# Second attention layer of a graph network: the wait for the sums moved behind ScalarE's distances

## The reference, cut to what matters

```python
q = (h @ Wq + bq).reshape(n, HEADS, HEAD_DIM) * scaling
k = (h @ Wk + bk).reshape(n, HEADS, HEAD_DIM)
v = (h @ Wv + bv).reshape(n, HEADS, HEAD_DIM)
s = jnp.einsum('ehd,ehd->eh', q[row], k[col])
m = jax.ops.segment_max(s, row, num_segments=n)
p = jnp.exp(s - m[row])
denom = jax.ops.segment_sum(p, row, num_segments=n)
attn = p / denom[row]
out = jax.ops.segment_sum(attn[:, :, None] * v[col], row, num_segments=n)
```

## Time and profile before

| | |
|---|---|
| median of 3 runs | 9040.61 us (9038.01 to 9045.36) |
| profiled execution, its own time | 9037.91 us |
| its span, first to last instruction | 9036.1 us |
| busy share of the span | PE 69%, DVE 63%, ACT 27%, POOL 68% |
| mean granted TensorE clock over the span | 0.809 of full speed |
| second attention layer, first to last one-hots (L1469) | 5319.6 to 7633.4 us |

### The profile page before, as it was taken

The page is one execution under the profiler, slowest core; times in us unless marked ns, Lnnn a source line. Parts: engine busy times, 40 slices in busy tenths (PEclk is TensorE's granted clock), DMA queues, the critical chain, the costliest instruction groups (busy, mean ns, idle before and its releaser), DMA issues. The chain is left out here.

```text
span 9036.1 us, 124148 instructions
## 1 busy us (share of the span) xinstructions
PE 6249.3 (69%) x27682; PEld 3822.4 (42%) x27683; DVE 5729.5 (63%) x14736; ACT 2476.3 (27%) x7366; POOL 6125.2 (68%) x5632
## 2 busy tenths in 40 slices
PE   5100077777777775999999778888888887555554
PEld 2000044444444444444444445555555555334433
DVE  7000076666666665888888778888888887322223
ACT  0000044444444442333333223333333333000000
POOL 4777677777777774888888635555555555677772
PEclk8555577777777777999999889999999998777776
DMA  2000043333343342333233533333333344333354
GB/s 88 13 1 1 8 117 104 107 106 106 107 108 108 108 106 60 86 84 85 84 85 85 53 94 105 105 105 105 105 105 106 105 106 92 98 104 104 105 99 50
DMA packets 411759, 790.73 MB, mean 88 GB/s; under 512 B 198754, under 2 KB 228172, under 8 KB 411084
## 3 DMA queue, kind: packets, MB, share of 16 engines
q0 software_dynamic: 283584, 725.19, 31.8%
q1 hardware_dynamic: 128140, 65.15, 2.5%
HBM read 749.73 MB, written 40.22 MB: 87 GB/s over the span
## 5 line engine op out<-in xcount | busy, mean ns | idle before, releaser
L1787 POOL DMA_INDIRECT gat<-y,rec_sb_s x908 | 1218.7, 1342 | 276.5 <-issue 259.4
L1545 DVE TENSOR_REDUCE small<-ps 128x2 f32<-128x1024 f32 x900 | 1091.7, 1222 | 308.1 <-PE ps L1413 266.4
L907 POOL DMA_INDIRECT gat<-kv,rec_sb_d x912 | 988.3, 1084 | 302.1 <-issue 275.2
L1350 POOL DMA_INDIRECT gat<-kv,rec_sb_s x916 | 889.9, 971 | 403.6 <-issue 314.3
L2051 POOL DMA_INDIRECT gat<-x,rec_sb_d x908 | 863.1, 951 | 332.2 <-issue 265.0
L2065 PE MATMUL ps<-gat,oh 128*128 128x256 f32 x1792 | 664.4, 537 | 528.7 <-DMA gat<-x,rec_sb_d 402.5
L495 POOL DMA_INDIRECT rec_s<-wts,rows x784 | 836.5, 1067 | 238.9 <-issue 238.3
L434 POOL DMA_INDIRECT rec_d<-small x784 | 764.9, 976 | 335.2 <-issue 247.2
L1828 PE MATMUL ps<-big,oh 128*128 128x512 f32 x1792 | 960.7, 635 | 0.0
L1360 POOL TENSOR_TENSOR big<-gat,big 128x1024 f32<-128x1024 f32 x225 | 442.6, 1967 | 588.4 <-ACT big L1483 588.4
L989 PE MATMUL ps<-big,oh 128*128 128x264 f32 x1800 | 795.3, 558 | 0.4
(11 more groups left out here) (276 smaller groups left out, 13812.2 us busy)
## 6 DMA issues: line engine op xcount, KB each, us to landing
gat<-kv,rec_sb_s POOLq DMA_INDIRECT x916
gat<-kv,rec_sb_d POOLq DMA_INDIRECT x912
rec_sb_s<-rec_s SPq DMA_DIRECT2D x456, 32.0 KB, 1.8
gat<-y,rec_sb_s POOLq DMA_INDIRECT x908
gat<-x,rec_sb_d POOLq DMA_INDIRECT x908
kv<-big SPq DMA_DIRECT2D x52, 256.0 KB, 2.0
rec_d<-small POOLq DMA_INDIRECT x784
rec_s<-wts,rows POOLq DMA_INDIRECT x784
```

The source lines that it names most:

```text
L907: e.indirect_dma_start(out=gat[:, m.u, q, :], out_offset=None, in_=table, in_offset=bass.IndirectOffsetOnAxis(ap=r_sb[:, m.u, q, 0:1].bitc ...
L1350: e.indirect_dma_start(out=gat[:, m.u, q, :], out_offset=None, in_=table, in_offset=bass.IndirectOffsetOnAxis(ap=r_sb[:, m.u, q, 0:1].bitc ...
L1545: V.tensor_reduce(mx[:, 2 * pair:2 * pair + 2], psH[pair % 2], AX.X, ALU.max).then_inc(s_hr, 1)
L1787: e.indirect_dma_start(out=rows_y[m.u][:, q, :], out_offset=None, in_=y1, in_offset=bass.IndirectOffsetOnAxis(ap=r_sb[:, m.u, q, 0:1].bitc ...
```

## The change

In `one_hots` of the second attention layer, the wait for the sums of macro m-4 moves from ahead of the four distances to just ahead of the `Relu` that writes `oh`. The wait for the record stays where it was, and so does everything else.

```diff
             def one_hots(e, m):
                 e.wait_ge(s_rec[m.u], m.turns(16))
-                e.wait_ge(s["sum"], m.done(U))
                 for q in range(Q):
                     last = A.activation(away[:, q, :], iota[:, :], ACT.Abs, scale=-1.0, bias=r_sb[:, m.u, q, 1:2])
                 last.then_inc(s["far"], 1)
                 e.wait_ge(s["far"], m.done())
+                e.wait_ge(s["sum"], m.done(U))
                 A.activation(oh[:, m.u, :, :], away, ACT.Relu, scale=-1.0, bias=1.0).then_inc(s["oh"], 1)
```

## The result

The changed kernel takes 8676.58 us (median of 4 runs, 8668.52 to 8682.01) against 9039.31 us for the kernel before in the same comparison: a ratio of 0.9598 (95% interval 0.9581 to 0.9614), 363 us faster. The forecast was 8725 us in a range from 8705 to 8815. The direction was right, and so was most of the mechanism; the gain was larger than the range allowed.

What follows compares the result with a forecast made beforehand. The prediction took a loop through PE, waiting for ACT's late one-hots, plus half-clocked stretches as the bound. Saving 0.74 (wait) and 0.67 (clock) us over 224 turns, 316 us, gave 8722, adjusted to 8725 us, range 8705 to 8815.

Steps and rivals of the forecast that it cites:

- The distances are covered: On ACT, the four distances end 0.94 us before PE's sums are done, so their 1.28 us is wholly hidden.
- PE's wait goes, L1380 follows L1420 by itself: PE's 1.16 us wait for the one-hots vanishes; L1380 starts 0.91 us after L1420, 1.31 us earlier.
- DVE is next: DVE becomes the bound: node scores are ready some 0.57 us before it can take them; PE waits ahead of L1400.
- The clock stays up: PE's granted clock stays at 2.4 GHz through the layer, since the idle time next to L1420 goes.
- the 0.67: The part of the 1.41 us gain a turn that was put down to the half-clocked stretches.
- two kinds of turn: Full-clock turns of 9.57 us alternate with turns of 11.14 us that hold a half-clocked stretch of 3.40 us.
- DVE's turn is 8.83 us: DVE's own work from first reduction to the next, read from an existing turn with its wait cut out: 8.83 us.
- one wait: DVE's wait for PE's node scores ahead of its first reduction, 0.59 us in the full-clock turn shown.
- The sum: Over the second attention layer, 10.24 - 8.83 = 1.41 us a turn, times 224 turns, saves 316 us.
- The range: Eight in 10 for the kernel's time: 8705 to 8815 us, taking in the case of a falling clock.
- a clock that would go on falling: Rival: DVE-bound, but PE's clock in the layer falls as now; saving 235 us, time 8806 us, chance 0.13.

Runs made afterwards that it cites:

- The kernel with the held loads: On the changed kernel, DVE's first reduction and bucket-number loads wait until `add_sums` of the turn before has ended; ratio 0.9772 in both sets.
- The filler: On the kernel before, nine unread bf16 matmuls of 192 columns put between L1420 and L1380, in PE's wait for the one-hots; ratio 0.9859.

## Why the prediction was right and where it was wrong

- *The distances are covered*: right. They ended 1.06 us before the sums (forecast 0.94).
- *PE's wait goes, L1380 follows L1420 by itself*: right, 0.92 us behind it (forecast 0.91, read from the layer's first turn).
- *DVE is next*: right. It is busy for 97% of the layer's stretch, its wait for L1413 is gone, and PE waits ahead of L1400 instead (97 us in 149 turns, up to 0.7 us). The kernel with the held loads shows it best: 0.43 us more on DVE lengthened the turn by about as much. But PE is close behind: when DVE's order was changed, its wait for PE's maxima at edges took over and the kernel got slower.
- *The clock stays up*: right, 1.00. The filler isolates it: about 140 us, forecast 0.67 x 224 = 150. Not all of the 0.67 is the clock. The prediction had two kinds of turn alternate; the trace has three, of 224 turns 93 of 9.58 us, 44 of 9.85 (at most one in each pass of four) and 87 of 11.15. The 9.85 ones are worth 0.05 us a turn; they stay with the filler and are gone in the changed kernel, for a reason that wasn't looked for. The trace agrees with the rule of the Trainium skill's page "TensorE: Matmul & The Clock Gate", section "A second HAM failure mode: psum-queue depth-cycling", that short idle spells can make the clock swing: PE's wait here was 1.2 us at the longest.
- *DVE's turn is 8.83 us*: wrong, and this is the step that failed. The forecast said of DVE's own work that it "has no wait on PE that the move could lengthen" and cut out its "one wait" only. It did not ask what the wait was holding up. Behind it in DVE's program stood the register loads of the bucket numbers, and their 0.3 us between the first two reductions, marked "issue" in the trace, was a consequence of the wait. With the node scores ready early, the sequencer starts the loads while DVE is still at work, and the gap closes. 8.83 - 0.31 is 8.52, the turn shown above took 8.56 by the starts of L1531 (6400.42 to 6408.98 in its timeline), and the mean was 8.63, 0.20 below the forecast.
- *The sum*: 1.61 us a turn instead of 1.41, 361 us instead of 316.
- *The range*: its low end was too near, since the gaps in DVE's turn were taken to be its own. The prediction named 8.62 us, DVE's busy time, as the lower bound of its turn, and that gives 9040.6 - 1.62 x 224 = 8678 us, where the result is. This is luck. The 8.62 is the busy time of one stretch of 9.60 us, and it is no floor. The turn shown took 8.56 us, with DVE busy for 8.37 of it:

```profile
6397.74:6406.30 8.56, 8.37 (x53) 5.34 (x52) 8.37 (x15) 3.69 (x10) 5.79 (x6) 1.00 0.44 125
```

  Two instructions that follow each other without a gap overlap by some 0.1 us in the records, as in the row of 2.35 us for two reductions of 1.22 and 1.23, so the busy time itself shrinks as gaps close. The high end of the range was held open for a clock that would go on falling, of which nothing came.

## What to carry to other kernels

When a wait is taken away, look at what stands right behind it in the waiting engine's program for its sequencer alone (register loads, computed addresses): such work can be exposed only because the engine was held, and then it vanishes together with the wait. A gap marked "issue" soon behind a wait can be a mark of it; let the range of the forecast include the turn without that gap. Where PE idles for a while in every turn, look at the granted clock: here it cost nearly as much as the wait itself (0.6 and 0.7 us a turn). Price it by a turn at each level, and test it with matmuls that nobody reads. And put the unaltered kernel beside every variant: a difference of 96 us shrank to 25 because the unaltered kernel had a delay of its own in that set.

## What the runs showed of the hardware that was not expected

- Two register loads and the work around them take DVE's sequencer about 1.3 us (6385.9 to 6387.2), and they run beside the engine's own instructions. With the sequencer held until `add_sums` has ended, the starts of two reductions of 1.22 us are 1.44 us apart, and 1.13 without.
- Nine matmuls a turn that do nothing useful, in a wait of 1.16 us, kept the granted clock at 1.00 (0.94 without them, in the comparison) and made the kernel before faster by 1.4%.
- A turn that was shorter at full clock (9.48 instead of 9.57 us) brought nothing (ratio 1.0007), while the share of the time at half clock was 16% where the comparison had 12% (granted clock 0.92 and 0.94).
- The same kernel's layer took 1952.5 to 2061.1 us in different sets, with a signal from L1420 that reached DVE up to 0.6 us later than its records suggest. Two sets with the same chip number differed too. The cause is open.
